# Second attention layer: one PSUM bank per step for factors and edge rows, and maxima subtracted by TensorE

## The reference

```python
q = (xn @ Wq + bq).reshape(n, H, DH)
k = (xn @ Wk + bk).reshape(n, H, DH)
v = (xn @ Wv + bv).reshape(n, H, DH)
ep = ef @ We + be
scores = jnp.einsum('ehd,ehd->eh', q[dst], k[src] + ep[:, None, :]) * scale
scores = scores * ew[:, None]
m = jax.ops.segment_max(scores, dst, num_segments=n)
ex = jnp.exp(scores - m[dst])
s = jax.ops.segment_sum(ex, dst, num_segments=n)
attn = ex / s[dst]
out = jax.ops.segment_sum(attn[:, :, None] * v[src], dst, num_segments=n)
```

## Time and profile before

| | us |
|---|---|
| median of 3 runs | 7708.78 (7702.34 to 7718.29) |
| the profiled execution | 7700.1, span 7698.3 |
| DVE busy | 4813.3 (63%) |
| PE busy | 5516.4 (72%) |
| ACT busy | 3689.0 (48%) |
| POOL busy | 5189.0 (67%) |

### The profile page before, as it was taken

How to read it: one execution, slowest core, us unless ns; L and a number is a source line. 1 busy time by engine, 2 the same in 40 slices (tenths; PEclk the granted TensorE clock), 3 DMA queues, 4 the chain that set the end, 5 groups by cost and what they waited for, 6 DMA issues and landing times. The chain is left out here.

```text
span 7698.3 us, 119086 instructions
## 1 busy us (share of the span) xinstructions
PE 5516.4 (72%) x30906; PEld 4168.8 (54%) x30906; DVE 4813.3 (63%) x14290; ACT 3689.0 (48%) x11072; POOL 5189.0 (67%) x5181
## 2 busy tenths in 40 slices
PE   6777666555569899967888888797555555767664
PEld 5666665555546566644666666564433434545443
DVE  8666666666658788877999999311222224555555
ACT  1333333222247777754888888342000003777774
POOL 4777777777777777743777776202777773777773
PEclk9777777777789999988999999898777777888886
DMA  4333341111145666645777776313444444444443
GB/s 147 79 79 82 77 110 34 37 34 34 36 112 156 159 156 159 158 119 151 200 200 197 204 200 167 111 58 94 109 109 108 109 108 73 109 110 110 109 110 87
DMA packets 1041596, 885.35 MB, mean 115 GB/s; under 512 B 749049, under 2 KB 857617, under 8 KB 1040823
## 3 DMA queue, kind: packets, MB, share of 16 engines
q0 software_dynamic: 259600, 658.46, 31.6%
q1 hardware_dynamic: 726977, 162.08, 11.0%
q10 hardware_dynamic: 54374, 57.20, 2.2%
HBM read 736.38 MB, written 140.99 MB: 114 GB/s over the span
## 5 line engine op out<-in xcount | busy, mean ns | idle before, releaser
L1302 POOL DMA_INDIRECT edges_kv<-kv,edges_rec x1712 | 1849.7, 1080 | 579.9 <-issue 484.4
L1449 PE MATMUL banks<-edges_kv,edges_hot 128*128 128x288 f32 (+2 forms) x5136 | 1478.4, 436 | 314.2 <-DVE edges_kv L1785 224.0
L1449 PEld LDWEIGHTS banks<-edges_kv,edges_hot 128*128 128x128 f32 x5136 | 1015.4, 208 | 581.0 <-issue 330.8
L1978 POOL DMA_INDIRECT edges_rows<-rel,edges_rec x856 | 809.5, 946 | 382.2 <-issue 256.5
L574 POOL DMA_INDIRECT by_src_records<-sort_by_src_rec,sort_by_src_pos_i x808 | 793.6, 982 | 325.7 <-issue 226.8
L1302 POOL DMA_INDIRECT edges_kv<-feat,edges_rec x856 | 828.4, 968 | 268.4 <-issue 242.2
L1994 PE MATMUL banks<-edges_rows,edges_hot 128*128 128x256 f32 x1712 | 624.9, 529 | 467.9 <-DMA edges_rows<-rel,edges_rec 424.3
L574 POOL DMA_INDIRECT by_dst_records<-sort_by_dst_rec,sort_by_dst_pos_i x808 | 789.1, 977 | 246.4 <-issue 242.4
L661 DVE SCALAR_TENSOR_TENSOR sort_junk<-banks,sort_hot_lo 128x128 bf16<-128x128 f32 x1616 | 438.9, 289 | 653.5 <-PE banks L723 640.2
L1994 PEld LDWEIGHTS banks<-edges_rows,edges_hot 128*128 128x128 f32 x1712 | 430.4, 263 | 662.8 <-DMA edges_rows<-rel,edges_rec 270.3
L1605 ACT ACTIVATE edges_off<-columns,edges_column 128x128 bf16<-128x128 f32 x2568 | 785.7, 394 | 0.0
(11 more groups left out here) (456 smaller groups left out, 11854.4 us busy)
## 6 DMA issues: line engine op xcount, KB each, us to landing
edges_kv<-kv,edges_rec POOLq DMA_INDIRECT x1712
sort_feat<-in_edge_attr_dram SPq DMA_DIRECT2D x100, 256.0 KB, 4.1
rel<-tables_stage SPq DMA_DIRECT2D x100, 252.0 KB
by_dst_records<-by_dst_blank ACTq DMA_DIRECT2D x21, 800.0 KB
edges_rec<-by_dst_records SPq DMA_DIRECT2D x26, 592.0 KB, 8.0
by_src_records<-by_src_blank ACTq DMA_DIRECT2D x1, 13696.0 KB, 52.5
edges_rows<-rel,edges_rec POOLq DMA_INDIRECT x856, 2.7
edges_kv<-feat,edges_rec POOLq DMA_INDIRECT x856
```

The lines of the kernel that those rows point to most:

```text
L1302: pool.indirect_dma_start(kv[:, r, c, 0:koff + DIM], None, tab, bass.IndirectOffsetOnAxis(ap=reci[:, b, c, idx:idx + 1], axis=0)).then_inc ...
L1449: last = pe.matmul(ps[:, 6 + m % 2, 0:OW], hot[:, b % 2, c, :], kv[:, b % BUFS, c, koff:koff + OW], start=(c % 2 == 0), stop=(kind != 1 an ...
L1978: pool.indirect_dma_start(rows[:, r, c, :], None, tab, bass.IndirectOffsetOnAxis(ap=reci[:, b, c, idx:idx + 1], axis=0)).then_inc(gathered ...
```

## The change

Two PSUM banks, 0 and 4, alternate by step. In its bank a step has the penalties' product and later the turned-back factors (columns 0 to 127), the turned scores (128 to 255) and, new, a copy of its edge rows `ep` (256 to 511). Code for the other layers keeps its banks.

```diff
+    SHARED = (0, 4)
+    EXP_AT = {0: 3 * P, 1: 0, 3: 2 * P}[kind]
...
+                def subtract(j, b):
+
+                    pe.wait_ge(scanned, at(j, b)(2, 2))
+                    pe.matmul(ps[0:HG, SHARED[b % 2], P:2 * P], minus[:], seg_max[:], start=False, stop=True, skip_group_check=True
+                              ).then_inc(below_done, 1)
...
                     if ahead and kind == 1:
                         pe.wait_ge(front_copied, at(*ahead)(1, 1))
+                        pe.wait_ge(ep_ready, at(*ahead)(1, 1))
...
                     if oldest:
                         sums(*oldest, 0)
-                        if kind == 1:
-                            with_past(*oldest, 0)
+                    if older and kind == 1:
+                        subtract(*older)
+                    if oldest and kind == 1:
+                        with_past(*oldest, 0)
...
+                    if kind == 1 and not first_steps(j, b, 2):
+                        act.wait_ge(below_done, n(1, 0) - 1)
                     if not first_steps(j, b, 3):
                         act.wait_ge(max_kept, n(1, 0) - 2)
...
+                def edge_rows(j, b):
+
+                    act.copy(ps[:, SHARED[b % 2], 2 * P:4 * P].rearrange("p (c d) -> p c d", c=G), rec[:, b, :, 0:dh]).then_inc(ep_ready, 1)
...
-                    act.activation(expo[:], below[:], ACT.Exp).then_inc(exp_done, 1)
+                    act.activation(expo[:], ps[0:HG, SHARED[b % 2], P:2 * P] if kind == 1 else below[:], ACT.Exp).then_inc(exp_done, 1)
...
-                        front(*ahead)
+                        if kind != 1:
+                            front(*ahead)
                         hot_rows(*ahead, 0)
...
                     if older:
                         exponentials(*older)
+                    if ahead and kind == 1:
+                        front(*ahead)
                     if oldest:
-                        move_sums(*oldest, (0, 1))
+                        move_sums(*oldest, (0,))
+                    if ahead and kind == 1:
+                        edge_rows(*ahead)
+                    if oldest:
+                        move_sums(*oldest, (1,))
...
+                    if kind == 1 and not first_steps(j, b, 1):
+                        dve.wait_ge(below_done, n(1, 0))
                     dve.tensor_tensor_scan(seg_max[:, ::-1], behind[:, 1:P + 1][:, ::-1], run_max[:, ::-1], -BIG,
                                            ALU.add, ALU.max).then_inc(scanned, 1)
...
-                    dve.tensor_tensor(below[:], sc_t, seg_max[:], ALU.subtract).then_inc(below_done, 1)
+                    if kind != 1:
+                        dve.tensor_tensor(below[:], sc_t, seg_max[:], ALU.subtract).then_inc(below_done, 1)
...
-                    if kind == 3:
-                        exps = ps[:, 0, 2 * P:2 * P + HG].rearrange("p (c h) -> p c h", h=H)[:, t]
+                    if kind > 0:
+                        exps = ps[:, exp_bank(b), EXP_AT:EXP_AT + HG].rearrange("p (c h) -> p c h", h=H)[:, t]
...
-                        ep = rec[:, b, t, 0:dh].unsqueeze(2).to_broadcast([P, 4, H, dh])
+                        if h == 0:
+                            dve.wait_ge(ep_ready, n(1, 1))
+                            if not first_steps(j, b, 2):
+                                dve.wait_ge(tail_copied, n(1, 0) - 1)
+                        rows = ps[:, SHARED[b % 2], 2 * P:4 * P].rearrange("p (c d) -> p c d", c=G)
+                        ep = rows[:, t].unsqueeze(2).to_broadcast([P, 4, H, dh])
```

More of the change, by code:

```diff
@@ L1120, in edge_layer, with score_at, exp_bank @@
     LO_BANKS = {0: (5, 5), 1: (3, 3), 3: (3, 2)}[kind]
-    SEG_BANK = {1: 0, 3: 5}.get(kind)
-    SCORE_AT = (0, 2 * P) if kind == 0 else (4, P)
-    EXP_AT = 3 * P if kind == 0 else 2 * P
+    SHARED = (0, 4)
+    EXP_AT = {0: 3 * P, 1: 0, 3: 2 * P}[kind]
+    def score_at(b):
+        return {0: (0, 2 * P), 1: (SHARED[b % 2], P), 3: (4, P)}[kind]
+    def exp_bank(b):
+        return SHARED[b % 2] if kind == 1 else 0
     UNROLL = 12
@@ L1197, in edge_layer @@
         pair_sums = ph.sbuf("pair_sums", [P, HELD, PAIRS, OW])
+        if kind == 1:
+            minus = ph.sbuf("minus", [HG, HG])
         if kind == 0:
@@ L1242, in edge_layer @@
         keyed = ph.sem("keyed")
+        ep_ready = ph.sem("ep_ready")
         scanned = ph.sem("scanned")
@@ L1344, in front @@
                         pe.wait_ge(tail_copied, n(1, 1) - 3)
-                    pe.matmul(ps[0:HG, SEG_BANK, 0:P], seg_wide[:].rearrange("p g h -> p (g h)"), C.to_next[:],
+                    pe.matmul(ps[0:HG, SHARED[b % 2] if kind == 1 else 5, 0:P], seg_wide[:].rearrange("p g h -> p (g h)"), C.to_next[:],
                               start=True, stop=True).then_inc(front_turned, 1)
@@ L1409, in turn_scores @@
                     if not first_steps(j, b, 1):
-                        pe.wait_ge(below_done, n(1, 0))
+                        if kind != 1:
+                            pe.wait_ge(below_done, n(1, 0))
                         if kind == 0:
@@ L1413, in turn_scores @@
                     pe.sem_inc(turns_begun, 1)
-                    bank, c0 = SCORE_AT
+                    bank, c0 = score_at(b)
                     pe.transpose(ps[0:HG, bank, c0:c0 + P], score[:].rearrange("p g h -> p (g h)"), C.ident[:]).then_inc(score_turned, 1)
+                def subtract(j, b):
+                    pe.wait_ge(scanned, at(j, b)(2, 2))
+                    pe.matmul(ps[0:HG, SHARED[b % 2], P:2 * P], minus[:], seg_max[:], start=False, stop=True, skip_group_check=True
+                              ).then_inc(below_done, 1)
                 def turn_back(j, b):
@@ L1429, in turn_back @@
                     pe.sem_inc(turns_begun, 1)
-                    pe.transpose(ps[:, 0, EXP_AT:EXP_AT + HG], expo[:], C.ident[0:HG, 0:HG])
-                    bank, c0 = (7, OW) if kind == 0 else (0, EXP_AT + HG)
+                    pe.transpose(ps[:, exp_bank(b), EXP_AT:EXP_AT + HG], expo[:], C.ident[0:HG, 0:HG])
+                    bank, c0 = (7, OW) if kind == 0 else (exp_bank(b), EXP_AT + HG)
                     pe.transpose(ps[:, bank, c0:c0 + HG], last_max[:], C.ident[0:HG, 0:HG]).then_inc(exp_turned, 1)
@@ L1587, in front @@
                         return
+                    if kind == 1 and not first_steps(j, b, 2):
+                        act.wait_ge(below_done, n(1, 0) - 1)
                     if not first_steps(j, b, 3):
                         act.wait_ge(max_kept, n(1, 0) - 2)
[L1590 removed]
+                    act.mul(pen[:, b % 3, 1:P], ps[0:HG, SHARED[b % 2] if kind == 1 else 5, 1:P], BIG).then_inc(front_copied, 1)
+                def edge_rows(j, b):
+                    act.copy(ps[:, SHARED[b % 2], 2 * P:4 * P].rearrange("p (c d) -> p c d", c=G), rec[:, b, :, 0:dh]).then_inc(ep_ready, 1)
                 def penalties(j, b):
@@ L1629, in tails @@
                     act.copy(kv[:, b % BUFS, :, koff + DIM:koff + OW].rearrange("p c (i h) -> p i c h", i=2),
-                             ps[:, 0, 2 * P:2 * P + 2 * HG].rearrange("p (i c h) -> p i c h", i=2, c=G)).then_inc(tail_copied, 1)
+                             ps[:, exp_bank(b), EXP_AT:EXP_AT + 2 * HG].rearrange("p (i c h) -> p i c h", i=2, c=G)).then_inc(tail_copied, 1)
                 def move_sums(j, b, pairs):
@@ L1662, in _ @@
                     penalties(0, 0)
+                if kind == 1:
+                    edge_rows(0, 0)
                 for h in range(2):
@@ L1707, in _ @@
                 dve.memset(pen[:], -BIG).then_inc(dve_set, 1)
+                if kind == 1:
+                    dve.tensor_scalar(minus[:], C.ident[0:HG, 0:HG], -1.0, None, ALU.mult)
                 if kind > 0:
```

## The result

| | before | after |
|---|---|---|
| median, us | 7710.37 (4 runs, 7702.34 to 7718.29) | 7759.96 (4 runs, 7756.52 to 7763.67) |
| span of the profiled execution, us | 7698.3 | 7757.9 |
| median step of the stage, us | 11.30 | 11.85 |

The changed kernel is slower: ratio 1.0066, 95% interval 1.0054 to 1.0078, 49.6 us between the medians. The steps are medians of 84 to 98 in each trace, 95 before and 90 after, from one copy 0 to the next, between about 3650 and 4740 us. 0.55 us in each of 105 steps is 58 us, close to the 59.6 us by which the profiled spans differ. The medians differ by 10 us less, since the profiled execution of the kernel before (7700.1 us) lies 10.3 us under its median and the one after lies at its median. The granted clock of TensorE in 3650 to 4740 us is 1.00 in both traces, the 2.4 GHz level, so the clock has no part in the difference.

A forecast was written before the change was run, and what follows sets the result against it. The prediction took a loop of PE and ACT waiting for each other as the bound; 0.39 us x 105 steps = 41 us on 7700.1 gave 7741, or a median of 7750 us, range 7705 to 7778 us.

The forecast's parts named there:

- The bound: Steady stage: PE and ACT wait for each other in a loop, 4.88 + 4.77 + 1.69 = 11.34 us, the whole step.
- DVE's subtraction at nothing: DVE, between scans and second key addition: losing 0.28 us a step gains nothing, taken in by the wait before the product.
- the PSUM inputs at nothing: Four large DVE operations a step reading one input from PSUM: 0 to 0.1 us a step won, all hidden.
- The subtraction on PE at 0.25 us: PE, between first sums and past 0: the added product makes past 0 end 0.25 us later; bounds 0.22 and 0.36.
- ACT's exponential and register load behind it, 0.39 us in all: ACT before copy 0: exponential waits for PE's subtraction, penalties and register load follow, so copy 0 starts 0.39 us later.
- The sign named for this wait: Profile after, ACT before copy 0: idle time no longer ended by past 0 alone, exponential starting behind the subtraction.
- the other signs: Copy 1–2 and 0–1 unchanged; DVE's product wait 0.5 us or more; gathers near 0.95 us; POOL waiting over 1 us.
- The edge rows and the second load under copy 1's wait at nothing: ACT between copies 0 and 1: edge-row copy, about 0.4 us, and register load hidden under the 0.91 us wait.
- DVE as the pace: Rival, whole step: DVE limits it, 0.38 us a step saved, 7669 us; chance 0.14 together with POOL's rival.
- POOL as the pace: Rival, gathers: POOL limits the step and is freed until DVE stops it, 7669 us; chance 0.14 together with DVE's rival.
- The nearly hidden subtraction: Rival, past 0 or copy 0: unseen slack leaves 0.1 to 0.2 us a step, 7719 to 7730 us; chance 0.16.
- The wait on the factor copy as a loop: Rival, DVE's first key addition: waiting for the factor copy may add 0.2 us to the forecast's step, 7771 us; chance 0.08.

The follow-up runs named there:

- Experiment 4: Kernel before plus an unused 64x64 zero product on PE between the first sums and past 0, nothing waiting for it: 7770.73 against 7710.71 us, ratio 1.0078.
- experiment 3: Changed kernel with PE's subtraction behind the fourth expand pair, ACT's exponential, penalties and edge rows between copies 0 and 1: 7704.88 us, ratio 0.9993 to kernel before.
- Experiment 6: Kernel before with ACT's copy 2 behind the third of eight one-hot instructions instead of the eighth: 7746.04 against 7720.30 us, ratio 1.0034.
- 7: Changed kernel with the subtraction late on PE, exponential, penalties and edge rows behind copy 0, and copy 2 early: 7827.98 us, ratio 1.0143 to kernel before.
- experiment 8: Changed kernel with late subtraction, early copy 2, and the fourth expand pair ahead of the first sums: 7868.29 us, ratio 1.0192 to kernel before.
- 1: Kernel before with only the subtraction moved to PE; one bank, edge rows and factors from SBUF: 7765.89 against 7710.71 us, ratio 1.0072.
- experiment 2: Changed kernel with the subtraction back on DVE, everything else of the change kept: 7707.56 us, ratio 0.9990 to kernel before.
- experiment 5: Kernel before plus an unused zero product with 128x128 weights between the first sums and past 0: 7750.85 against 7720.30 us, ratio 1.0041.
- experiment 9: Kernel before with three of ACT's eight one-hot instructions moved between copy 0 and copy 1, no copy moved: 7691.32 against 7715.14 us, ratio 0.9969.

## Why the prediction was right

**The bound.** Right, and shown. The loop of PE and ACT was read from two waits and three pieces of the timeline; two of the three are unchanged to 0.01 us after the change, and the third carries the loss. Experiment 4 puts work into it that nobody needs and pays in full; experiment 3 moves the same product out and pays nothing.

It was not complete. The second one-hot is another way through the same loop, with about 0.19 us to spare, and I did not see it, since it ends (3913.05) before the sums without making a wait of its own. Experiment 6 failed on it, and 7 and 8 in part.

**DVE's subtraction at nothing, the PSUM inputs at nothing.** Right: experiments 1, 2 and 4. The operations became 0.02 to 0.03 us shorter, in the bounds of 0 to 0.1 us a step for all four. The rule of the Trainium skill that would have made them longer by 0.065 us (VectorE: DVE Perf Modes, section The TRN2 errata) is contradicted once more, at a median of 1210 ns with an input in PSUM against 1217 ns without. DVE's wait before the last pair's product was forecast at 0.5 us or more and is 1.06 us.

**The subtraction on PE at 0.25 us.** Too low; this is the term that was mis-sized. Measured are 0.57 us at the end of past 0 in the step shown and 0.55 us a step. That is above both bounds of the forecast, 0.22 and 0.36 us: it took the columns alone, and set aside the row that would have given 0.36 us from the start of one to the start of the next, because the stream has no wait. A product of 128x128 weights costs the 0.22 us of the columns (experiment 5); the other 0.33 us come with the 64x64 weights: by the medians of 91 to 94 steps in experiments 4 and 5, 0.09 us before the product, 0.14 us between it and past 0, 0.10 us in past 0 itself. The first and the last stand in no term of the forecast.

**ACT's exponential and register load behind it, 0.39 us in all.** Wrong as a mechanism. Copy 0 starts 0.18 us behind past 0 after the change as it did before, so ACT's sequencer had caught up by then. Experiment 4 has the loss without this wait. The sum of 41 us came near the 49.6 us by luck, because a path that does not bind was given 0.14 us more than the one that does, and that one was 0.30 us too cheap. With the mechanism right and the product at 0.25 us the sum would have been 26 us. The sign named for this wait did not come: ACT's idle time before copy 0 is still ended by past 0. The step (11.85 us) and copy 2 to copy 0 (5.28 us) lie a little above the 11.6 to 11.8 and 5.1 to 5.2 us that were named; the other signs came.

**The edge rows and the second load under copy 1's wait at nothing.** Right: 0.37 us where about 0.4 us was estimated, 1.69 us from copy 0 to copy 1, and experiment 2.

**The rivals.** DVE as the pace: refuted by 1 and 4, where DVE's work went down and stayed, with the same step. POOL as the pace: refuted by 2, where the gathers fall from 1109 to 946 ns and the step stays at 11.30 us. The Trainium skill (SBUF — State Buffer, section Who interferes with whom) is borne out as far as the gathers go: the longest took 2079 ns before and 991 ns after, where no large DVE operation has two inputs in SBUF. The nearly hidden subtraction: refuted by 4. The wait on the factor copy as a loop: it did not bind in the changed kernel (no such wait in its list), but DVE waited 128.7 us for that copy in experiment 8.

## What to carry to other kernels

Where two engines wait for each other every step, write the loop down piece by piece; work put into a piece was paid in full here and work beside it was free, and moving the same instruction by two places in PE's order, with the work that follows it on ACT, was the difference between 50 us and nothing. Look also at what ends just before a piece starts without making a wait, because it is the next limit as soon as something is moved. An engine that gets lighter pays only when the loop that holds it has been opened: here the change cost 50 us alone, and with two one-hot instructions and the subtraction in other places the same work was 39 us faster than before. Of these 39 us the kernel before got 24 us from its own one-hot instructions moved (experiment 9), without the change.

## What the runs showed of the hardware

A product with 64x64 weights in a stream of 128-row products cost more than one with 128x128 weights and the same columns: 0.55 against 0.22 us a step (experiments 4 and 5). In the trace the matmul after it comes 0.36 us behind its start and not 0.22, and the pair that follows takes 0.72 us and not 0.62. The loads of the weights show a difference that goes with this: those of the 64x64 product and of past 0 behind it start with their matmuls (0.00 us ahead in the median of 91 steps), those of the 128x128 product 0.23 us ahead and of past 0 behind it 0.11 us ahead. Why the smaller weights are not loaded ahead is not settled; only the two sizes were run, and rows and columns were changed together.
